# Seventeen matmuls whose result nobody reads, and a two-column GELU, between the two stages of a one-core transformer block

## The reference

```python
x = x + tanh(g_xattn[0]) * xattn(layernorm(x), ctx, ctx, mask, ...)   # 16 heads of 8
x = x + tanh(g_ffn[0])   * ffn(layernorm(x), ...)

def ffn(x):                                    # x: 4096 x 128
    gate = softmax(x @ Wg + bg)                # 4096 x 8
    thr = sigmoid(x @ Wt + bt) * 0.125
    w = maximum(gate - thr, 0); w = w / (sum(w) or 1)
    h = gelu(einsum('td,edf->etf', x, W1) + b1)    # 8 experts, 128 -> 512
    eo = einsum('etf,efd->etd', h, W2) + b2        # 512 -> 128
    return einsum('te,etd->td', w, eo)
```

## Time and profile before

| | us |
|---|---|
| median of 3 runs | 675.88 (674.58 to 676.32) |
| the profiled execution | 674.14 |
| its span, first to last instruction | 672.3 |
| PE busy | 639.3 (95%) |
| DVE busy | 543.5 (81%) |
| ACT busy | 434.3 (65%) |

### The profile page before, as it was taken

How to read it: one execution, slowest core, us unless ns; L and a number is a source line. 1 busy time by engine, 2 the same in 40 slices (tenths; PEclk the granted TensorE clock), 3 DMA queues, 4 the chain that set the end, 5 groups by cost and what they waited for, 6 DMA issues and landing times.

```text
span 672.3 us, 14393 instructions
## 1 busy us (share of the span) xinstructions
PE 639.3 (95%) x3988; PEld 486.5 (72%) x3988; DVE 543.5 (81%) x1088; ACT 434.3 (65%) x764; POOL 186.2 (28%) x240
## 2 busy tenths in 40 slices
PE   7899999999999999739999999999999999999997
PEld 6566666767766666427878878788788788787886
DVE  6788888889888888345888888888888888888886
ACT  4566666666666666417766766667667667676663
POOL 7334444444444442100221221211212212212121
PEclk9999999999999999959999999999999999999999
DMA  4544444444444444104111112112121121121120
GB/s 128 149 125 122 122 121 121 121 121 121 126 122 126 117 109 110 42 0 77 49 45 62 44 48 63 48 47 62 47 62 47 47 62 47 47 62 47 47 62 16
DMA packets 39887, 52.80 MB, mean 79 GB/s; under 512 B 9520, under 2 KB 23728, under 8 KB 39856
## 3 DMA queue, kind: packets, MB, share of 16 engines
q1 hardware_dynamic: 39856, 52.42, 28.2%
HBM read 26.58 MB, written 2.23 MB: 43 GB/s over the span
## 4 chain that ended last, share of the span: by engine, by line
PE 86%; DVE 7%; DMA 2%; issue 2%; ACT 2%; SPq 1%; POOL 0%; DVEq 0%; ACTq 0%; POOLq 0%
PE ps_h L1114 9%; PE ps_y L1094 9%; PE ps_y L1095 9%; PE ps_y L1096 9%; PE ps_h L1116 9%; PE ps_h L1115 9%; PE scores L1042 5%; PE scores L1043 4%; PE scores L1050 4%; PE scores L1051 3%; PE heads L1061 3%; DVE neg_max L681 3%; PE misc L926 2%; PE misc L927 2%; PE misc L928 2%
## 5 line engine op out<-in xcount | busy, mean ns | idle before, releaser
L645 ACT ACTIVATE h_sb<-ps_h,b_sb 128x512 f32<-128x512 f32 x256 | 176.3, 690 | 109.1 <-PE ps_h L1116 95.6
L870 DVE TENSOR_TENSOR h_low<-h_sb,h_high 128x512 fp32r<-128x512 f32 x256 | 164.3, 682 | 0.0
L866 DVE CAST h_high<-h_sb 128x512 fp32r<-128x512 f32 x128 | 98.5, 769 | 68.6 <-ACT h_sb L645 68.6
L536 POOL TENSOR_TENSOR yT<-yT,weighted 128x512 f32<-128x512 f32 x54 | 69.7, 1291 | 301.3 <-DVE weighted L858 301.3
L1114 PE MATMUL ps_h<-x_high,w_high 128*128 (+1 forms) x256 | 103.2, 403 | 1.7 <-ACT h_sb L645 1.6
L1094 PE MATMUL ps_y<-h_high,w_high 128*128 128x512 f32 x256 | 101.6, 397 | 0.8 <-DVE h_low L870 0.8
L1095 PE MATMUL ps_y<-h_low,w_high 128*128 128x512 f32 x256 | 101.5, 396 | 0.0
L1096 PE MATMUL ps_y<-h_high,w_low 128*128 128x512 f32 x256 | 101.1, 395 | 0.0
L1115 PE MATMUL ps_h<-x_low,w_high 128*128 (+1 forms) x256 | 100.3, 392 | 0.0
L1116 PE MATMUL ps_h<-x_high,w_low 128*128 (+1 forms) x256 | 100.2, 391 | 0.0
L681 DVE TENSOR_REDUCE neg_max<-scores 128x4 f32<-128x512 f32 x128 | 83.4, 685 | 10.2 <-PE scores L1051 9.3
(11 more groups left out here) (133 smaller groups left out, 1007.0 us busy)
## 6 DMA issues: line engine op xcount, KB each, us to landing
w_row<-w_scratch SPq DMA_DIRECT2D x64, 256.0 KB, 3.1
k_masked<-k_stack SPq DMA_DIRECT2D x64, 128.0 KB, 2.4
k_cur<-k_stack SPq DMA_DIRECT2D x16, 512.0 KB, 3.0
q_masked<-q_stack SPq DMA_DIRECT2D x64, 96.0 KB
w_raw<-in_w_ffn SPq DMA_DIRECT2D x16, 256.0 KB, 2.7
ctx_sb<-in_ctx SPq DMA_DIRECT2D x16, 128.0 KB, 2.1
out_y<-y_out SPq DMA_DIRECT2D x7, 256.0 KB, 2.3
x_all<-in_x SPq DMA_DIRECT2D x13, 128.0 KB, 2.4
```

Of the source, the lines that this page charges most:

```text
L645: nc.scalar.activation(h_sb[:, j % HBUF, :], ps_h[:, j % 4, :], ACT.Gelu_apprx_tanh, bias=b1_sb[:, j:j + 1]).then_inc(h_done, 1)
L866: V.tensor_copy(h_high[:, j % HBUF, :], h_sb[:, j % HBUF, :]).then_inc(high_odd, 1)
L870: V.tensor_tensor(h_low[:, j % HBUF, :], h_sb[:, j % HBUF, :], h_high[:, j % HBUF, :].bitcast(F32), ALU.subtract).then_inc(low2_done, 1)
```

## The change

Two insertions, nothing removed. On ACT, behind the two exponentials of the gate and ahead of the two copies, a GELU of a 128x2 tile (`tanh_g`, made at the start) into two columns of `power`, which nobody reads any more. On PE, behind the last matmul of stage A and ahead of the wait for `g_dve` 15, waits for `x2_high` and for stage A's readers of `scores`, and then 17 matmuls of `x2_high` by itself, 128x512 each, into buffer 0 of `ps_h`. The first real matmul of stage B starts that buffer anew.

```diff
@@ scalar
             nc.scalar.activation(g_exp[:], g_exp[:], ACT.Exp).then_inc(g_act, 1)
             nc.scalar.activation(g_thr[:], logits[:, :, E], ACT.Exp, scale=-1.0).then_inc(g_act, 1)
+            act.wait_ge(tanh_done, 1)
+            nc.scalar.activation(power[:, 0:2], tanh_g[:], ACT.Gelu_apprx_tanh).then_inc(g_act, 1)
             for q in range(2):
                 act.wait_ge(g_full, q + 1)
@@ tensor
             loop(pe, body)
 
 
+            pe.wait_ge(x2high_done, NG)
+            for u in range(2):
+                pe.wait_ge(scoresT_read[u], NG * SLABS)
+                pe.wait_ge(scoresN_read[u], NG * SLABS)
+            for _ in range(17):
+                mm(ps_h[:, 0, :], x2_high[:, 0:P], x2_high[:, 0:BT], start=True, stop=True)
             pe.wait_ge(g_dve, 15)
```

## The result

| | before | after |
|---|---|---|
| median of 7 runs, us | 675.6 (673.39 to 676.32) | 671.57 (670.23 to 672.92) |
| the profiled execution, us | 674.14 | 671.77 |
| its span, us | 672.3 | 670.0 |

The ratio is 0.9948, with a 95% interval of 0.9932 to 0.9964: some 3.5 us less (2.4 to 4.6), faster by more than 0.3%. On the 675.88 from which the prediction was made, the ratio gives 672.4, against the 673.2 forecast, in a range of 672.0 to 675.2. The gain of 3.5 lies above the forecast's own 2.2 to 2.8; it is inside the range only because that had been widened downwards.

What follows compares the result with a forecast made beforehand. Stage B was taken as bound by PE, so an earlier start carries through: table load 1.28, first three matmuls 0.6, transposes 0.85, together 2.7 us, from 675.88 to 673.2 us; range 672.0 to 675.2.

Steps and rivals of the forecast that it cites:

- What bounds the kernel: From the first `ps_y` matmul PE hardly waits, so starting stage B earlier by d ends the kernel earlier by d.
- The table load: On ACT, moving the load from before the first GELU to behind the gate's exponentials takes 1.28 us off the chain.
- no drain: The Trainium skill's extra 1.38 us per table switch was not counted, as ACT had idled 0.76 us before the load.
- The clock's part: At the start of stage B, PE at full clock saves 0.85 us on transposes and 0.6 on the first three matmuls.
- When the clock comes up: PE's full clock returns at 296.6 to 298.1 us, with the 17 matmuls starting at about 293.25.
- The gap: Between the 17 matmuls and the transposes PE idles up to 1.1 us, and the clock was taken to hold.
- The road over DRAM: Gate weights' path to the first combine gains only 0.7 us; slack 1.1 us at worst, so no cost.
- The slow rival: The 17 matmuls outlast the gate, at 1.26 us each ending 14.9 us late; kernel some 688 us; chance 0.04.
- The size of the whole: Whole kernel: 2.7 us less, 675.88 to 673.2 us; the forecast had chance 0.76.

## Why the prediction was right, point by point

**What bounds the kernel.** Right. PE bounds stage B, and a start earlier by 2.7 us went through: from the first `ps_y` to the end it is 364.8, 364.7 and 364.5 us in the three traces of before, 364.4, 364.4 and 364.6 in those of the changed kernel.

**The table load.** Right to the hundredth: 1.28 us. The load and its small GELU sat in ACT's idle time and ended 4.0 us ahead of the copies. The reason given for counting no drain, that ACT had been idle ahead of the load, was not what decided: with the 17 matmuls alone ACT had just been at work, and the price was the same.

**The clock's part.** The size is right, 1.42 us. So are its pieces: transposes, copies and matmuls came at the distances given, the first GELU 1.92 us after the gate's end, where 301.6 - 299.71 = 1.9 had been forecast.

**When the clock comes up.** This step was wrong. I took 3.3 to 4.8 us after the start of work for the whole of what could be; the traces with 17 or 34 at the gate and a low clock before them gave 3.1, 3.2, 5.3, 5.6, 5.8 and 5.8. It cost nothing, since 17 at the mixed rates still ended by the gate's end, and that was luck in part. By the sum the 17 were over at 298.95, 0.8 us ahead of the transposes (the prediction calls this the issue of the last, which is one slot of 0.23 earlier). In the three traces of the changed kernel, with the same slot for the last, they were over some 0.05 to 0.15 us ahead. At the low clock alone they would have been late, by an estimate of half a microsecond (293.81 + 7.26 against 300.54).

**The gap.** Right: where the 17 ended early, the clock stayed at 1.00 through 1.1 us of idle PE. That is one trace.

**The road over DRAM.** Right that it costs nothing, with a slack of 4.2 us, much larger than the bound of 1.1.

**The slow rival.** What lies behind it, matmuls that outlast the gate, is real, as 34 of them show. Its price was wrong: a single one cost 0.427 at the low clock and 0.231 at the full one, as L1114 does, not what the idle turns on fp32 zeros do.

**The size of the whole.** Forecast 2.7; the runs gave 3.5, three times over (0.9948, 0.9948, 0.9951), each with an interval that holds 2.7. In the three traces of either kernel the mean spans are 672.8 and 669.9, 3.0 apart: 2.7 from the chain, 0.2 from stage B, 0.1 from stage A, where single executions vary by a microsecond and more. Most of the rest of 0.5 is that the three traced executions of before were short ones: the 61 timed executions of before beside the experiments have a mean span of 673.3 against the traces' 672.8, the 24 of the changed kernel 670.0 against 669.9. Whether the gain of the whole beyond the chain's 2.7 is chance or has a cause in executions that no trace caught stays open. The two first profiled executions alone would mislead, since their spans differ by 2.3 only: before had a short stage A, with the gate's end at 299.71 against 301.03 and 300.41 in its two other traces. The forecast is untouched by that, as it subtracts the chain's gain from the median of the runs.

## What to carry to other kernels

Between two stages, where one engine works in small dependent steps, the others' switches (a table load, a clock that has fallen) can be brought forward into the idle time, and their price is read straight off the chain: in this kernel the two added up to the hundredth in the traces. Size such fillers so that they end at the event they lead up to even if the clock comes up late: nine brought nothing of the clock's part in their trace, and what outlasted the event with 34 was paid in full. The return of the clock is not certain, as the 10.3 us at the low clock with a busy PE show, so look at more than one trace. Count both traces from the same event, since what ran ahead of it differs by more than the effect.

## What the runs showed of the hardware

While nine matmuls of 512 columns ran in a row the clock did not come up, in the one trace that there is; with 17 or 34 it did in all six traces, between 3.1 and 5.8 us after their start. In one trace PE was idle for 1.1 us between busy stretches and the clock stayed at 1.00. In two traces it stayed at 0.50 for 10.2 and 10.3 us near the kernel's start, with PE busy for 9.31 and 9.18 of them. A table load cost 1.28 us wherever it stood, 0.13 us behind other work of ACT as well as after idle time.
